# Swapped-half sine product in one VectorE instruction, and GpSimd halving the squares ahead of VectorE's sums

## What is computed

```python
q, k, v = split(shift_tokens(x) @ Wqkv)          # 16 heads of 64
q = q / max(norm(q), 1e-12) * q_scale            # per token and head
k = k / max(norm(k), 1e-12) * k_scale
q = q * cos * scale + rotate_half(q) * sin * scale     # rotate_half: [-x2, x1]
k = k * cos / scale + rotate_half(k) * sin / scale
x = softmax(local window of 32 + 32 keys)(q, k) @ v @ Wo + x
x = gated_ffn(layernorm(shift_tokens(x))) + x    # gelu gate, 341 wide
```

## Time and profile before

| | |
|---|---|
| median of 3 runs | 4228.52 us (4224.45 to 4230.75) |
| the profiled execution | 4228.07 us, of which the span is 4226.3 us |
| busy over the span: PE, DVE | 3943.4 us (93%), 3877.6 us (92%) |
| busy over the span: ACT, POOL | 2604.9 us (62%), 2692.1 us (64%) |
| mean granted TensorE clock | 0.991 |
| first and last start of `den` (L957), 192 turns | 999.37 and 4169.93 us |

### The profile page before, as it was taken

The page is one execution under the profiler, slowest core; times in us unless marked ns, Lnnn a source line. Parts: engine busy times, 40 slices in busy tenths (PEclk is TensorE's granted clock), DMA queues, the critical chain, the costliest instruction groups (busy, mean ns, idle before and its releaser), DMA issues. The chain is left out here.

```text
span 4226.3 us, 124870 instructions
## 1 busy us (share of the span) xinstructions
PE 3943.4 (93%) x48616; PEld 2737.1 (65%) x48616; DVE 3877.6 (92%) x4836; ACT 2604.9 (62%) x3780; POOL 2692.1 (64%) x4716
## 2 busy tenths in 40 slices
PE   7999999997999999999999999999999999999996
PEld 4666666665666666666666666666666666666664
DVE  5888888887899999999999999999999999999994
ACT  4666666653566666666666665666666666666663
POOL 5565556545667676676667666666676666666663
PEclk9999999999999999999999999999999999999999
DMA  5454554540000001000110001100011000010000
GB/s 136 93 100 94 98 98 93 103 98 20 24 17 15 20 29 29 17 15 17 31 29 16 16 16 30 29 18 15 16 30 29 20 15 16 20 38 20 15 16 14
DMA packets 342441, 165.08 MB, mean 39 GB/s; under 512 B 114241, under 2 KB 337473, under 8 KB 341185
## 3 DMA queue, kind: packets, MB, share of 16 engines
q1 hardware_dynamic: 342208, 161.99, 17.3%
HBM read 115.67 MB, written 33.69 MB: 35 GB/s over the span
## 5 line engine op out<-in xcount | busy, mean ns | idle before, releaser
L630 POOL TENSOR_TENSOR pn<-es,rden 128x1024 f32<-128x1024 f32 x192 | 366.3, 1908 | 695.3 <-DVE rden L959 695.3
L726 ACT ACTIVATE y<-ps 128x1024 f32<-128x1024 f32 x384 | 372.2, 1021 | 511.1 <-PE ps L1205 511.1
L634 POOL TENSOR_TENSOR t<-t 128x1024 f32<-128x1024 f32 x192 | 454.5, 2367 | 79.8 <-DVE t L911 79.8
L911 DVE TENSOR_TENSOR t<-ps,tabl 128x512 f32<-128x512 f32 x768 | 491.0, 681 | 0.0
L678 ACT ACTIVATE t<-ps,amx 128x512 f32<-128x512 f32 x512 | 347.5, 688 | 224.6 <-DVE amx L815 224.6
L909 DVE TENSOR_TENSOR t<-ps,tabl 128x1024 f32<-128x1024 f32 x384 | 467.2, 1217 | 8.0 <-ACT sq L749 4.3
L636 POOL TENSOR_TENSOR t<-t 128x1024 f32<-128x1024 f32 x192 | 452.8, 2358 | 4.4 <-DVE t L911 4.4
L1013 DVE TENSOR_TENSOR qn<-t,rn 128x2048 f32<-128x2048 f32 x192 | 438.1, 2282 | 5.6 <-POOL rn L399 5.6
L969 DVE TENSOR_REDUCE ss<-sq 128x32 f32<-128x2048 f32 x192 | 437.0, 2276 | 0.0
L1054 PEld LDWEIGHTS ps<-cst,qn 128*128 128x128 f32 x3072 | 350.2, 141 | 118.6 <-issue 61.7
L815 DVE TENSOR_REDUCE amx<-ps 128x2 f32<-128x1024 f32 x256 | 310.9, 1214 | 109.9 <-PE ps L1076 109.6
(11 more groups left out here) (134 smaller groups left out, 8224.5 us busy)
## 6 DMA issues: line engine op xcount, KB each, us to landing
wm<-values_dram SPq DMA_DIRECT2D x128, 256.0 KB, 5.1
y<-values_dram SPq DMA_DIRECT2D x128, 256.0 KB, 4.9
values_dram<-qT SPq DMA_DIRECT2D x64, 256.0 KB, 2.3
tokens_dram<-x SPq DMA_DIRECT2D x96, 128.0 KB
xs<-tokens_dram SPq DMA_DIRECT2D x192, 64.0 KB, 1.8
xw<-tokens_dram SPq DMA_DIRECT2D x192, 64.0 KB, 1.8
xsh<-x SPq DMA_DIRECT2D x48, 128.0 KB
xsh<-x SPq DMA_DIRECT2D x48, 127.0 KB
```

What stands on the lines that cost most here:

```text
L630: nc.gpsimd.tensor_tensor(heads(pn[:], H), heads(es[:], H), rden[:].unsqueeze(2).to_broadcast([P, H, KEYS]), ALU.mult).then_inc(l_p, 1)
L634: nc.gpsimd.tensor_tensor(t1[:, 0:INNER], t1[:, 0:INNER], t2[:, 0:INNER], ALU.add).then_inc(l_rotq, 1)
L726: return act.activation(y[:].rearrange("p h (w q) -> p w h q", w=NW)[:, 2 * half:2 * half + 2], src.rearrange("p (w h q) -> p w h q", w=2, ...
L911: sine = nc.vector.tensor_tensor(t23[:, :, lo:lo + DH // 2], q3[:, :, hi:hi + DH // 2], tabl[:, 1, u, i, lo:lo + DH // 2].unsqueeze(1).to_ ...
```

## The change

For each of q and k, the two sine products of 512 columns become one of 1024 columns, whose PSUM operand is read with the two halves of every head in reverse order. On POOL, two additions are put into every turn behind `pn` and ahead of the two `t1 + t2`: each waits for the squares of q or of k and adds, in place, the upper 32 squares of every head to the lower 32 (16 heads, 512 columns). DVE's sum waits for both of them on a new semaphore `l_sf`, and reads 32 columns of each head instead of 64, 1024 in all.

```diff
@@ POOL, turn
                     nc.gpsimd.tensor_tensor(heads(pn[:], H), heads(es[:], H),
                                             rden[:].unsqueeze(2).to_broadcast([P, H, KEYS]), ALU.mult).then_inc(l_p, 1)
                 if s.has(3):
+                    for half, squared in enumerate((l_sqq, l_sqk)):
+                        pool.wait_ge(squared, t + 4)
+                        sums = heads(sq[:, half * INNER:(half + 1) * INNER], H)
+                        nc.gpsimd.tensor_tensor(sums[:, :, 0:DH // 2], sums[:, :, 0:DH // 2], sums[:, :, DH // 2:DH],
+                                                ALU.add).then_inc(l_sf, 1)
                     pool.wait_ge(l_rq, t + 4)
                     nc.gpsimd.tensor_tensor(t1[:, 0:INNER], t1[:, 0:INNER], t2[:, 0:INNER], ALU.add).then_inc(l_rotq, 1)
@@ DVE, rotate
                 nc.vector.tensor_tensor(t13, q3, tabl[:, 0, u, i].unsqueeze(1).to_broadcast([P, H, DH]), ALU.mult)
-                for lo, hi in ((0, DH // 2), (DH // 2, 0)):
-                    sine = nc.vector.tensor_tensor(
-                        t23[:, :, lo:lo + DH // 2], q3[:, :, hi:hi + DH // 2],
-                        tabl[:, 1, u, i, lo:lo + DH // 2].unsqueeze(1).to_broadcast([P, H, DH // 2]), ALU.mult)
-                sine.then_inc(done, 1)
+                swapped = src.rearrange("p (h s d) -> p h s d", h=H, s=2)[:, :, ::-1, :]
+                nc.vector.tensor_tensor(t23.rearrange("p h (s d) -> p h s d", s=2), swapped,
+                                        tabl[:, 1, u, i].rearrange("p (s d) -> p s d", s=2).unsqueeze(1)
+                                        .to_broadcast([P, H, 2, DH // 2]), ALU.mult).then_inc(done, 1)
@@ DVE, turn
                     rotate(1, u, pool1, l_rk)
-                    nc.vector.tensor_reduce(ss[:], heads(sq[:], 2 * H), X, ALU.add).then_inc(l_ss, 1)
+                    dve.wait_ge(l_sf, (t + 4) * 2)
+                    nc.vector.tensor_reduce(ss[:], heads(sq[:], 2 * H)[:, :, 0:DH // 2], X, ALU.add).then_inc(l_ss, 1)
```

More of the change, by code:

```diff
@@ L283, in build @@
         l_sqk = sem("l_sqk")
+        l_sf = sem("l_sf")
         l_ss = sem("l_ss")
```

## The result

| | before | after |
|---|---|---|
| median | 4228.69 us (4224.45 to 4230.75, 4 runs) | 4553.83 us (4548.54 to 4557.21, 4 runs) |
| profiled execution, and its span | 4228.07, 4226.3 us | 4548.54, 4546.7 us |
| first to last start of `den` | 3170.56 us | 3486.73 us |
| mean granted clock | 0.991 | 0.972 |

The ratio is 1.0771 (95%: 1.0758 to 1.0784). The forecast was 4545 us, range 4440 to 4640. Of the 320.4 us that the span grew by, 316.2 lie between the first and the last `den`, so in the turns of the layers.

What follows compares the result with a forecast made beforehand. The prediction took the loop through POOL and DVE, not idle shares, as the limit: 7.25 us per batch item, 348 us over 48 items, less 29 of cover, on 4228.07 gives 4547, say 4545 us; range 4440 to 4640.

Steps and rivals of the forecast that it cites:

- The reading: In each turn, POOL's idle time counts only where it lies inside the loop, not as its 20 us per item.
- the loop: Chain in each turn through DVE and POOL: den, rden, `pn`, two sums, Newton, `qn`, next den; forecast 17.3 against 15.48 us.
- The three gaps of 1.17 us: POOL's idle gaps inside a c = 2 turn, 0.42, 0.34 and 0.41 us, claimed as all the room before the turn lengthens.
- The third gap: POOL's idle time between Newton's end at 12.80 us and `qn` at 13.21 in a c = 2 turn: 0.41 us.
- DVE's 4.33 us behind it: DVE's own work from the guess's end to `qn` in turns c = 2 and 3, putting `qn` at 15.03 us.
- The whole saving on DVE is spent waiting: DVE's 1.34 us less work per turn gains nothing, since floor and guess are held by POOL's sums.
- Floor and guess: DVE steps ahead of Newton: floor held to about 8.35 us, guess held by POOL's sum for k until 10.7.
- Rival B: POOL keeps the ports through both sums, floor waits until 10.7 us: 4590 us; 15% together with somewhat dearer additions.
- Rival A: POOL's own loop alone is the limit, the guess slipping between its instructions: 4500 us; 24% together with cheaper additions.
- Turns c = 0 and c = 1: Next `den` forecast at 19.0 us against 17.41 for c = 0, and 18.8 against 16.81 for c = 1.
- PE and ACT set nothing: PE ends its scores before DVE wants them, has 62.07 us of work in 72, waits more and sets nothing.
- The cover: New wait partly hidden in irregular turns where PE sets the length: half of 58 us, 29 us, taken off.

Runs made afterwards that it cites:

- e6: Changed kernel with each POOL addition over 16 columns of each head in place of 32, leaving out a quarter of the squares: 4382.86 us, ratio 1.037.
- e4: Changed kernel with DVE's floor and guess (and statistics in c = 0) moved behind the residual add and the transpose of the weights: 4520.43 us, ratio 1.0689.
- e2: Changed kernel with the two old sine products of 512 columns, so the additions alone: 4544.94 us, ratio 1.075.
- e3: Changed kernel with the additions written to an unread spare tile and DVE summing all 64 squares of every head: 4607.56 us, ratio 1.0897.
- e1: Kernel before with the merged sine product alone, no additions on POOL: 4222.73 us, ratio 0.9988.
- e5: Changed kernel with the addition for q moved ahead of POOL's `pn`, that for k staying behind it: 4443.62 us, ratio 1.051.
- e8: Kernel before with one POOL power operation on 32 columns in place of guess and twelve Newton steps: 4354.62 us, ratio 1.0299.
- e11: e9 with residual add and transpose of the weights put ahead of statistics, floor and guess on DVE: 4422.03 us, ratio 1.0462.
- e9: Changed kernel with the feed-forward's root moved into the layers' Newton chain in turns c = 0, its own twelve steps dropped: 4451.79 us, ratio 1.054.
- e10: Kernel before with the merged sine product and the feed-forward's root in the layers' Newton chain, no additions on POOL: 4196.57 us, ratio 0.9931.

## Why the prediction was right

**The reading held.** POOL's place in the loop, not its idle share, decided. Measured: additions 1.278 us (forecast 1.25), guess ending 10.63 us after `den` (10.7), turns c = 2 and 3 of 17.11 us (17.3), the item 72.02 us (72.4), 316.2 us from first to last `den` (319), the profiled execution 4548.54 us (4547, rounded to 4545).

**The room was read too large.** The three gaps of 1.17 us were "all that can be added"; by e6 and the changed kernel it was 0.7 to 0.9 us. The third gap, 0.41 us between Newton and `qn`, is still there in the turn after (2990.93 to 2991.28, 0.35 us), because DVE's own work from the guess to `qn` is longer than Newton. Only in e4, where that gap is closed, is the room 1.0 us (2.56 - 1.53). The sum of the prediction doesn't use the 1.17: it goes by the guess and DVE's 4.33 us behind it, which is why it wasn't hurt.

**"The whole saving on DVE is spent waiting"** is shown from two sides: e2 gives 0.29 us of DVE's work back in each turn and loses no time; e3 gives 1.05 us back and costs 0.28. In the kernel before, e1 takes 0.29 us away and gains 0.1%. The price of the loop is shown by e5 (place), e6 (size) and e8 (another lengthening, without any of the edits).

**Floor and guess.** The forecast that the floor is released between POOL's two sums and the guess held by the second came out to 0.1 us. The rule of the Trainium skill weighed there (SBUF — State Buffer, section "Who interferes with whom"), that the one who issues first keeps the shared ports for its whole instruction, agrees with this trace, with e3 and e6 as its other half: a floor issued after the sum for k has begun is held for its full length, 2226 and 2142 ns. Rival B had one correct observation, POOL's instructions overlapping by 0.03 us; the floor got in nevertheless.

**Rival A** was right on what comes next. Where the guess is made to cost nothing behind POOL's sum (e4), the loop of POOL alone holds the turn at 17.01 us, A's 17.0, and the late `pn` makes c = 1 the long one: 17.9 and 19.7 us for c = 0 and 1 (A: 17.0 and 20.5), 71.6 to 71.9 us for the item (A: 71.5). So the two limits are 0.1 us apart, and taking one away is worth 33 us. A's price for it was 45 us (4545 to 4500); the mechanism that it gave, the guess slipping in, did not occur.

**Turns c = 0 and c = 1 were mis-sized, in opposite directions.** Forecast 19.0 and 18.8; measured 20.7 and 17.1. Their sum, 37.8, is right, and not wholly by luck (e4 gives 37.6 with another split). What the forecast left out: behind the held guess and the statistics DVE's transpose of the weights is late (it ends at 3007.28). The timelines of PE, ACT and DVE in that turn, one behind the other:

```profile
3007.61 1.85 PE L1211 MATMUL ps<-pT,xw 32*128 32x512 f32 x8 [3.50 <-DVE pT L990]
3009.21 1.96 PE L1211 MATMUL ps<-pT,xs 32*128 32x512 f32 x8
...
3026.30 1.14 PE L1211 MATMUL ps<-pT,xw 32*128 32x512 f32 x8
```

```profile
3011.29 1.94 ACT L732 ACTIVATE y<-ps 128x1024 f32<-128x1024 f32 x2 [5.74 <-PE ps L1211]
3013.11 1.06 ACT L787 ACTIVATE es<-es 128x1024 f32<-128x1024 f32 x1
```

```profile
3010.21 2.28 DVE L1019 TENSOR_TENSOR qn<-t,rn 128x2048 f32<-128x2048 f32 x1
3014.20 1.22 DVE L962 TENSOR_REDUCE den<-es 128x16 f32<-128x1024 f32 x1 [1.71 <-ACT es L787]
...
3031.28 1.22 DVE L962 TENSOR_REDUCE den<-es 128x16 f32<-128x1024 f32 x1
```

PE idles 3.50 us; the granted clock falls from 1.00 to 0.50, the 1.2 GHz level, and the two value products take 1.85 and 1.96 us, where 1.14 and 1.04 is what they take one turn on. ACT's copies and the exponential follow, and `den` waits 1.71 us for them. POOL, however, is late in any case, as its timeline behind that turn shows:

```profile
3014.55 1.04 POOL L655 TENSOR_TENSOR xnT<-xnT,frn 128x512 f32<-128x512 f32 x1 [0.16 <-POOL xnT L651]
3015.79 1.91 POOL L631 TENSOR_TENSOR pn<-es,rden 128x1024 f32<-128x1024 f32 x1 [0.20 <-DVE rden L964]
```

The forecast had it start 22.1 us into the turn, with `den` at 19.0 and 3.1 us ahead of it. It starts at 3015.79, 22.3 us into it; `den` is at 20.7, 1.6 us ahead, so the lost time is POOL's and is merely booked one turn earlier. e4 shows the same with PE's clock at 1.00: `den` at 17.9 us, `pn` at 22.15. "PE and ACT set nothing" was wrong for where a turn ends and right for the sum. Four items in a row of the fifth layer show the trade: with turns c = 0 of 20.1, 20.3, 20.5 and 20.7 us come turns c = 1 of 17.5, 17.3, 17.1 and 17.1. And e11, which has no drop of the clock but POOL's chain shorter by twelve steps, has that `pn` 19.7 us into the turn, not 22.3.

**The cover** for irregular turns was taken as 29 us. 48 items at the measured 6.84 us are 328 us, and 316 were lost, so it was 12: most of it in the second item of each layer, which lost 5.3 us, the others 6.1 to 7.5, and 4 us of it only because the count ends at the last `den`, three turns into the last item. In the second PE also folds the next weights. The turn was estimated 0.4 us per item too long and the cover 17 us too large; these errors, 20 us and 17 us, cancel.

What stays open: that PE sets the regular turn before is read and not tested; why e6 lies 0.26 us above its expected turn is read from the floor's hold and was not tested by itself; and why the clock falls behind PE's wait in one of e9's items and not in the next is not shown.

## What to carry to other kernels

Before work goes to an engine that looks idle, mark in one turn the waits that go out of it and come back: only its gaps inside that loop are room, and their sum is an upper bound (here 1.17 us a turn by the trace and 0.7 to 0.9 by the runs, where POOL idles for 5.1). e5 shows that the same instruction is half as dear where the engine would have waited. An instruction whose mean grows tenfold while its size stays is a wait in disguise; look for what runs beside it, and test by giving the engine more to do. If nothing gets slower (e2), shorten the loop elsewhere: dropping a second chain of short steps (e10, with the merged sine product) was worth 0.7%, the trade of work between engines minus 7.7%.

## What the runs showed of the hardware

- A POOL power operation on 32 columns took 5.46 us, more than the twelve Newton steps on the same columns with their gaps (3.84 us). POOL's additions took 1.278 us for 512 columns and 0.738 for 256. The estimate from the Trainium skill (GPSIMD Engine Reference, "Performance versus the Vector engine"), 1.11 us for 512, is below this, and the measurement decides.
- A DVE instruction with one SBUF input and 32 columns was held until the end of a POOL instruction that had begun 0.14 us before it, 2.28 us where it takes 0.18; so was a four-column one in e11's turn, for the 0.86 us that were left. The `qn` of that turn, 2048 columns, took 0.84 us longer where a POOL pass had started 0.07 us before it.
- Reading the two halves of every head in reverse order out of PSUM cost nothing in these 1024 columns: 1215 ns against 1217 for the straight order.
- Behind 3.50 us without work PE's granted clock fell from 1.00 to 0.50. Behind 2.27 us in e9 it was 0.64 in one item and 1.00 in the next, so the length of the wait alone did not decide it.
